# Causal mask added by VectorE in PSUM, and a layer norm with its turnings in two halves

## The reference

```
xn = (x - mean) / sqrt(var + 1e-05)
att = q @ k.T / sqrt(HD);  att = where(key > query, -inf, att);  y = softmax(att) @ v
x = x + (y @ wo) * silu(moe0(xn))          # layer 0
xn = layernorm(x)
x = x + delta_rule(xn) * silu(moe1(xn))    # layer 1
```

## Time and profile before

| what | value |
|---|---|
| median of 3 runs | 1938.27 us (1934.45 to 1939.06) |
| the profiled execution | 1930.35 us, span 1928.6 us |
| busy PE, DVE, ACT, POOL | 92%, 74%, 51%, 37% of the span |
| mean granted TensorE clock | 0.974 |
| ACT's idle time before the exponentials of attention | 17.8 us until a mask matmul, 12.9 us until a score matmul, 9.0 us unnamed |

### The profile page before, as it was taken

The page is one execution under the profiler, slowest core; times in us unless marked ns, Lnnn a source line. Parts: engine busy times, 40 slices in busy tenths (PEclk is TensorE's granted clock), DMA queues, the critical chain, the costliest instruction groups (busy, mean ns, idle before and its releaser), DMA issues.

```text
span 1928.6 us, 43598 instructions
## 1 busy us (share of the span) xinstructions
PE 1774.4 (92%) x14838; PEld 1284.5 (67%) x14838; DVE 1421.1 (74%) x2477; ACT 987.0 (51%) x2680; POOL 705.1 (37%) x870
## 2 busy tenths in 40 slices
PE   4578888899889999999999999999999999999997
PEld 3236665333545568777787787787877877877776
DVE  5776775111477578888888888888888888888887
ACT  1002223788522246566666565565665756656664
POOL 5640001120040224263362552643624616426334
PEclk9779998999989999999999999999999999999999
DMA  6725664010022310100100001001001010010010
GB/s 255 227 92 175 191 185 132 26 31 13 1 82 73 96 48 13 44 33 11 44 7 37 33 11 44 33 11 44 33 11 44 0 44 33 11 44 33 11 55 22
DMA packets 76374, 112.43 MB, mean 58 GB/s; under 512 B 24332, under 2 KB 57756, under 8 KB 73122
## 3 DMA queue, kind: packets, MB, share of 16 engines
q1 hardware_dynamic: 72810, 102.95, 16.1%
q0 software_dynamic: 3072, 8.39, 1.4%
q10 hardware_dynamic: 446, 0.48, 0.1%
HBM read 86.22 MB, written 28.73 MB: 60 GB/s over the span
## 4 chain that ended last, share of the span: by engine, by line
PE 55%; ACT 10%; issue 3%; DVE 3%; POOL 1%; DMA 0%; ACTq 0%; SPq 0%; POOLq 0%; DVEq 0%
PE ps L1344 9%; PE ps L1391 6%; PE ps L1401 4%; PE ps L1535 3%; PE ps L1638 3%; PE ps L1625 3%; PE ps L1640 3%; ACT gmask_Q L1780 2%; PE ps L1609 2%; PE ps L1614 2%; PE ps L1418 2%; PE ps L1428 2%; PE ps L1445 2%; PE ps L1597 2%; PE ps L1589 2%
## 5 line engine op out<-in xcount | busy, mean ns | idle before, releaser
L1860 POOL TENSOR_TENSOR kq_decayed<-conv,decay_rows 128x256 f32<-128x256 f32 x234 | 181.7, 801 | 452.2 <-PE ps L1638 452.2
L1989 DVE SCALAR_TENSOR_TENSOR conv<-raw,tap_st,conv 128x1024 f32<-128x1024 f32 x202 | 280.8, 1390 | 3.6
L1344 PE MATMUL ps<-xnT,w_conv_st 128*128 128x512 f32 x544 | 245.9, 596 | 0.0
L817 DVE TENSOR_REDUCE m_part<-ps 128x1 f32<-128x640 f32 (+7 forms) x176 | 176.1, 1027 | 67.8 <-PE ps L668 49.5
L1344 PEld LDWEIGHTS ps<-xnT,w_conv_st 128*128 128x128 f32 x544 | 98.2, 190 | 99.7 <-issue 94.9
L1020 ACT ACTIVATE probs<-ps 128x1024 f32<-128x1024 f32 (+1 forms) x192 | 142.1, 816 | 39.7 <-PE ps L944 17.8
L1401 PE MATMUL ps<-w_z_st,xnT 128*128 128x256 f32 x512 | 150.4, 396 | 0.0
L1659 ACT COPY raw<-ps 128x512 f32<-128x512 f32 x136 | 80.7, 593 | 123.3 <-PE ps L1344 122.5
L912 POOL DMA_INDIRECT slot_outputs<-scratch_slots_y,token_slots x32 | 30.4, 950 | 303.6 <-POOLq L497 207.4
L645 PE MATMUL ps<-k_stack,q_stack 128*128 128x512 bf16 (+3 forms) x384 | 103.3, 363 | 33.4 <-DVE m_part L817 18.1
L1391 PE MATMUL ps<-w_out_st,xn_nat 128*128 128x256 f32 x544 | 125.9, 384 | 6.9 <-ACT xn_nat L1692 6.9
(11 more groups left out here) (356 smaller groups left out, 4330.1 us busy)
## 6 DMA issues: line engine op xcount, KB each, us to landing
decay_rows<-scratch_egc SPq DMA_DIRECT2D x17, 1024.0 KB, 4.6
w_conv_st<-in_w_conv SPq DMA_DIRECT2D x17, 512.0 KB, 3.2
scratch_slots_x<-yacc SPq DMA_DIRECT2D x8, 1024.0 KB, 15.0
slot_rows<-scratch_slots_x SPq DMA_DIRECT2D x16, 512.0 KB, 4.9
scratch_slots_y<-slot_outputs SPq DMA_DIRECT2D x16, 512.0 KB, 3.7
w_gate_up<-in_gu SPq DMA_DIRECT2D x8, 768.0 KB
w_gate_up<-in_gu SPq DMA_DIRECT2D x32, 192.0 KB
k_nat_decayed<-in_gu SPq DMA_DIRECT2D x22, 256.0 KB, 2.8
```

What stands on the lines that cost most here:

```text
L817: dve.tensor_reduce(dst, src, AX.X, ALU.max).then_inc(s_max, 1)
L1344: mm = pe.matmul(ps[:, 6 + n % 2, :], wc[:, k, (n // 2) * P:(n // 2 + 1) * P], m.xnT[:, k, (n % 2) * HALF:(n % 2 + 1) * HALF], start=k == ...
L1860: op = g.tensor_tensor(kqe[:, e, :, at], cv[:, 0:2, at], egr[:, e, at].unsqueeze(1).broadcast_to([P, 2, P]), ALU.mult)
L1989: op = dve.scalar_tensor_tensor(out=cv[:, t, :], in0=raw[:, t, at:at + T], scalar=tap[:, t, at:at + 1], in1=cv[:, t, :], op0=ALU.mult, op1 ...
```

## The change

The mask matmul is taken out of PE's stream; a unit with a diagonal is finished by its score matmuls. DVE adds `future` to the first 128 columns of both banks in one operation of 128 x 2 x 128, in place in PSUM, and ACT's exponential of such a unit waits for that operation (`s_mk`) in place of PE. DVE's stream is laid out anew: the masks of each tile in order, the four operations that weight the expert outputs behind the masks of tiles 4 to 7 instead of at the start of the group, and the two masks of the next group's first tile ahead of the copy of this group's result.

The second layer norm runs in two halves of four chunks. DVE takes the statistics and aggregates of each half, POOL works on four columns at a time, and DVE normalises the first half behind the second half's aggregates. PE turns a half as soon as it is normalised, ACT copies 128x512 blocks, and the router matmuls of a half wait for its two blocks only. The first layer norm stays as it is.

```diff
+def dve_layer_norm_halves(dve, step, x, st, mv, xn, s_var, s_rstd, rstd):
+
+    for half in range(2):
+        of = range(half * NC // 2, (half + 1) * NC // 2)
+        for c in of:
+            step(dve.bn_stats(st[:, c, :], x[:, c, :]))
+        step.wait()
+        for c in of:
+            last = dve.bn_aggr(mv[:, c, :], st[:, c, :])
+        last.then_inc(s_var, 1)
+    for half in range(2):
+        dve.wait_ge(s_var, half + 1)
+        dve.wait_ge(s_rstd, half + 1)
+        for c in range(half * NC // 2, (half + 1) * NC // 2):
+            step(dve.tensor_scalar(xn[:, c, :], x[:, c, :], mv[:, c, 0:1], rstd[:, c:c + 1],
+                                   ALU.subtract, ALU.mult))
+
+def pool_rsqrt_var_halves(nc, pool, step, mv, rstd, minus_half, s_var, s_rstd):
+    for half in range(2):
+        of = slice(half * NC // 2, (half + 1) * NC // 2)
+        pool.wait_ge(s_var, half + 1)
+        step.link(nc.gpsimd.tensor_scalar(rstd[:, of], mv[:, of, 1], LN_EPS, None, ALU.add))
+        nc.gpsimd.tensor_tensor(rstd[:, of], rstd[:, of], minus_half[:, 0:1].broadcast_to([P, NC // 2]),
+                                ALU.pow).then_inc(s_rstd, 1)
...
-                                   m.qst[:, bass.ds(i * REP + 2 * pair + q, 1), at:at + w], start=True, stop=done > 0)
-                    if not done:
-                        mm = pe.matmul(ps[:, bank, 0:P], m.identb[:], m.future[:], start=False, stop=True)
+                                   m.qst[:, bass.ds(i * REP + 2 * pair + q, 1), at:at + w], start=True, stop=True)
...
-                        act.wait_ge(s_sc, i * UN + n + 1)
+                        if done:
+                            act.wait_ge(s_sc, i * UN + n + 1)
+                        else:
+                            act.wait_ge(s_mk, i * 2 * NC + 2 * kt + pair + 1)
...
+            def mask(i, kt):
+
+                for pair in range(REP // 2):
+                    n = unit(kt) + chunks(kt) * pair
+                    dve.wait_ge(s_sc, i * UN + n + 1)
+                    square = ps[:, 2 * (n % 3):2 * (n % 3) + 2, 0:P]
+                    dve.tensor_tensor(square, square, m.future[:].unsqueeze(1).broadcast_to([P, 2, P]), ALU.add).then_inc(s_mk, 1)
...
+            mask(0, 0)
             for i in range(NKV):
                 dve.wait_ge(s_pv, i * NC + 2)
                 dve.tensor_copy(vst[:], m.vaug[:, i, :, :]).then_inc(s_v, 1)
...
+                for kt in range(1, NC):
+                    mask(i, kt)
+                    if kt >= NC - TOP0:
+                        weigh(i, kt - (NC - TOP0))
+                if i + 1 < NKV:
+                    mask(i + 1, 0)
                 dve.wait_ge(s_pv, (i + 1) * NC + 2)
                 dve.tensor_copy(m.oT[:, i, :], ps[:, 6:8, :].rearrange("p b n -> p (b n)")).then_inc(s_o, 1)
...
-            pe.wait_ge(s_l1, 2 * NC)
-            for k in range(KT):
-                for c in range(NC):
-                    mm = pe.transpose(ps[:, 2 + 2 * k + c // 4, (c % 4) * P:(c % 4 + 1) * P],
-                                      m.xn[:, c, k * P:(k + 1) * P], m.ident[:])
-                mm.then_inc(s_tr, 1)
+            for half in range(2):
+                pe.wait_ge(s_l1, NC + (half + 1) * NC // 2)
+                for k in range(KT):
+                    for c in range(half * NC // 2, (half + 1) * NC // 2):
+                        mm = pe.transpose(ps[:, 2 + 2 * k + half, (c % 4) * P:(c % 4 + 1) * P],
+                                          m.xn[:, c, k * P:(k + 1) * P], m.ident[:])
+                    mm.then_inc(s_tr, 1)
             pe.wait_ge(in_r, 32)
-            pe.wait_ge(s_xnT, 2)
             for c in range(NC):
+                if c % 4 == 0:
+                    pe.wait_ge(s_xnT, KT + c // 4 * KT)
...
-            for k in range(KT):
-                act.wait_ge(s_tr, k + 1)
-                nc.scalar.copy(m.xnT[:, k, :], two_banks(2 + 2 * k)).then_inc(s_xnT, 1)
+            for half in range(2):
+                for k in range(KT):
+                    act.wait_ge(s_tr, half * KT + k + 1)
+                    nc.scalar.copy(m.xnT[:, k, half * HALF:(half + 1) * HALF], ps[:, 2 + 2 * k + half, :]).then_inc(s_xnT, 1)
```

More of the change, by code:

```diff
@@ L886, in stage_attention @@
                                               sem("yT_made"), sem("s_made"), sem("dve_steps"))
-        s_mixed = sem("pair_mixed")
+        s_mixed, s_mk = sem("pair_mixed"), sem("unit_masked")
         block = ctx.enter_context(nc.Block())
@@ L1033, in _, with weigh @@
             dve.sem_inc(s_o, 1)
+            def mask(i, kt):
[4 more added lines that the diff above has]
+                    dve.tensor_tensor(square, square, m.future[:].unsqueeze(1).broadcast_to([P, 2, P]), ALU.add).then_inc(s_mk, 1)
+            def weigh(i, n):
+                if n == 0:
+                    dve.wait_ge(s_got[i % 2], 16 * TOP0 * (i // 2 + 1))
+                    step.link(dve.tensor_scalar(m.yacc[:, i, :], got[:, i % 2, 0, :], m.wsel[:, i, 0:1], None, ALU.mult))
+                    return
+                op = dve.scalar_tensor_tensor(out=m.yacc[:, i, :], in0=got[:, i % 2, n, :], scalar=m.wsel[:, i, n:n + 1],
+                                              in1=m.yacc[:, i, :], op0=ALU.mult, op1=ALU.add)
+                if n < TOP0 - 1:
+                    step.link(op)
+                else:
+                    op.then_inc(s_mix, 1)
+            mask(0, 0)
             for i in range(NKV):
@@ L1874, in _ @@
             g.memset(w3f.rearrange("p c s -> p (c s)"), 0.0).then_inc(s_zero, 1)
-            pool_rsqrt_var(nc, pool, l1, m.mv, m.rstd, m.minus_half, s_lnv, s_lnr)
+            pool_rsqrt_var_halves(nc, pool, l1, m.mv, m.rstd, m.minus_half, s_lnv, s_lnr)
             pool.wait_ge(s_l1, 2 * NC)
@@ L2077, in _ @@
             beta = m.beta[:, 0:NV, :]
-            dve_layer_norm(dve, l1, m.x, m.st, m.mv, m.xn, s_lnv, s_lnr, m.rstd)
+            dve_layer_norm_halves(dve, l1, m.x, m.st, m.mv, m.xn, s_lnv, s_lnr, m.rstd)
             dve.wait_ge(in_w, 64)
```

## The result

The changed kernel takes 1925.04 us in the median of six runs (1920.01 to 1929.53), the kernel before 1936.26 us in six beside them (1933.76 to 1939.06). The ratio is 0.9938, 95% interval 0.9924 to 0.9952: 12.0 us faster, between 9.3 and 14.7. I had forecast 4.7 us, and named faster as the likeliest side. So the side is right and the size is about two and a half times the forecast.

The account below looks back on a forecast made before the run. Attention was taken as a PE-ACT-PE chain, the second layer norm as one serial chain, with PE the bound afterwards. Masks 0.8 plus layer norm 3.9 gave 4.7 us, from 1938.27 to 1933.6 us; range 1925 to 1941.

Parts of the forecast that it names:

- the rival with the shorter stall: First group of heads: four fewer gathers in a row shorten ACT's 8.37 us stall by 5.0 us, 1928.6; chance 0.25.
- The likeliest case: Whole kernel: masks 0.8 us plus layer norm 3.9 us, 4.7 us faster, 1933.6 us; chance 0.42.
- The layer norm, -3.9 us: Second layer norm in halves: router matmuls end at 542.15 in place of 546.04, 3.9 us earlier.
- The collision: Layer norm: first-half normalisations on DVE wait for POOL's second power over shared ports, costing about 0.5 us.
- The shift at 546 us: After the layer norm, rival: later DVE routing or weights eat some 3 of the 3.9 us, 1937; chance 0.08.
- The masks, -0.1 us a group: Attention: masks moved from PE to DVE gain 0.1 us a group, 0.8 us over eight.
- the detour: Masked units go PE, DVE, ACT: 0.51 us in place of a direct 0.04, 0.47 us extra latency.
- the end of the group: Attention, after the trades at tiles 5 to 7: PE is about 0.45 us ahead.
- The last step: Change of groups: the next group's first masked unit gives 0.47 - 0.11 us back.
- My slope for a longer detour: Attention: detour stands three times in a group's path, so each further 0.1 us costs 0.3 us a group.
- an addition of 0.68 us: Rival of a long detour: PSUM addition takes 0.68 us, attention loses 7 us, kernel 1941.7; chance 0.15.
- The rival of a falling clock: Attention: PE's clock drops from small waits, about 10 us more per group wholly at 1.2 GHz, 1943; chance 0.05.

Follow-up runs that it names:

- 1: Kernel before with only the second layer norm in halves, attention as before; ratio 0.9960 (0.9944 to 0.9975).
- 9: Kernel before with 39 added turnings of the identity on PE ahead of the second layer norm's turnings; ratio 0.9979 (0.9962 to 0.9997).
- 12: Kernel before, unchanged, profiled a second time; first projection 18.17 us after the statistics, no timed ratio given.
- 2: Kernel before with only the masks on DVE and the later weighting, serial second layer norm; ratio 0.9968 (0.9950 to 0.9987).
- 6: Kernel with masks on DVE and serial layer norm, plus a second addition ahead of each mask addition; ratio to the kernel before 1.0070 (1.0042 to 1.0099).
- 7: Kernel with masks on DVE and serial layer norm, but key tile 0's masks back on PE; ratio to the kernel before 0.9968 (0.9949 to 0.9988).
- 8: Changed kernel with the first eight gathers moved to the second group and weighting one group later; ratio to the kernel before 0.9938 (0.9909 to 0.9968).
- 3: Kernel before, masks on PE, with each chunk's weighting made to wait for its group's fourth product; ratio 1.0060 (1.0042 to 1.0077).
- 4: Changed kernel with four gathers in a row at the start in place of eight; ratio to the kernel before 0.9901 (0.9883 to 0.9918).
- 10: Changed kernel with four gathers in a row at the start and key tile 0's masks on PE; ratio to the kernel before 0.9888 (0.9865 to 0.9910).
- 11: Changed kernel with four gathers in a row, key tile 0's masks on PE and 24 turnings ahead of the layer norm's; ratio to before 0.9865 (0.9843 to 0.9886).
- 5: Kernel before without any mask, neither mask matmuls nor additions, exponential's scale divided by 256; ratio 0.9923 (0.9902 to 0.9945).

## Why the prediction was right on the side and wrong on the size

The measured 1925.04 us lies at the lowest edge of my range, the edge that I had drawn for the rival with the shorter stall, and 8.6 us below the 1933.6 of my sum. Of these 8.6 us 2.0 are the kernel before itself (1938.27 in three runs, 1936.26 in six). The rest comes from three terms of the sum that were too small, all to the same side, less 1.7 us that the sum did not have.

**The likeliest case left the first group as it was: the largest miss.** The step that failed is that my sum took this gain at nothing. I had it as the rival with a chance of 0.25 and 5.0 us. Measured, the first group went from 30.57 to 26.05 us, of which 0.34 belongs to the masks, so 4.2 us belong to the gathers. The length of the row decides: twelve gathers with masks on PE give holes of 8.37, 9.77, 8.46 and 8.37 us (before, 1, 9, 12), eight give 3.92, 3.87, 3.54, 3.91 and 3.66 with masks on DVE (after, 2, 6, 7, 8) and 4.19 with masks on PE (3), some with a second wait of about 2 us behind them, and four at a group's start give none (4, 10, 11). Without any mask twelve gave 5.23 and 2.73 us (5). Against the rival I had held that gathers ran without harm before 335 and that later sets of four cost nothing. Both are true and neither excludes it: the row begins with attention, and ACT gets on for 7 us before it stops. How gathers hold PE is not settled. The trace of after records the product of the first tile at 339.72 us and the scores behind it, for which ACT waits, at 341.57, but ACT gets them at 345.52. What holds them back in between no view shows. PE in time order, kernel after:

```profile
339.72 1.93 PE L955 MATMUL ps<-probs,v_stage 128*32 128x512 f32 x16
341.57 1.15 PE L968 MATMUL ps<-q_stack,k_stack 128*128 x6
```

**The layer norm, -3.9 us: right against one execution, too small against the kernel.** The pair of profiles gives -4.3. But my price of the serial form was a single execution's. When the clock rises behind the idle stretch differs from profile to profile, and the serial form is exposed to it. In its four profiles without masks on DVE (before, 3, 5, 12) the router takes 3.76 to 5.34 us and the projection comes 16.8 to 18.2 us after the statistics, 17.8 in the mean. In five of the halves (without 11) it is 4.1 to 4.5 and 12.3 to 12.8, 12.6 in the mean. That is -5.2 us. The step that failed is the one that took the 546.04 us of one execution, with "some 4.5 us" of low clock read from one mean of 0.68, as the serial form's end. The three serial profiles with masks on DVE (2, 6, 7) are slower still: each has its router at a clock of 0.50 throughout, 7.07 us, and its projection after 20.1 or 20.2 us. Whether the masks have a part in that, or three executions were unlucky, is not shown.

The clock is the cause of these differences: the same 32 matmuls take 3.76 us where it is 1.00 (before, 9) and 7.07 where it is 0.50 (2, 6, 7). In number 9, with PE at work in the idle stretch, the turnings run at the upper level as well, and the projection comes 2.6 us ahead of the mean of those four (15.2 to 17.8). Why the clock rises late in the serial form and not in the halves was not tried alone; PE idles 11.6 to 11.9 us in the one and 8.1 to 8.4 in the other.

Inside it the terms held: a power over four columns 1.06 and 1.04 us (I took 0.94), PE's start 4.86 us after the statistics (5.44 forecast), the projection 12.52 (12.93). The collision for which I counted 0.5 us did not come. Four normalisations took 1.36 us in a row from 534.46 while POOL's second power ran from 535.03. The Trainium skill, "SBUF — State Buffer", section "Who interferes with whom", says that when a VectorE operation in a 2-port mode meets a GpSimd operation, whichever issues first holds the shared ports for its whole instruction. The earlier trace rows bore that out beside a memset; beside a power of 128x4 these rows show no such block, and the measurement decides. In which mode a normalisation ran no view tells.

**The shift at 546 us is not eaten.** Against the profile of before 1.0 us was given back, and I had taken that for the cost of a later routing chain. Over the same four and five profiles the rest of the kernel takes 1384.0 us in the mean behind the serial form and 1383.4 behind the halves: nothing is given back.

**The masks, -0.1 us a group: measured -0.34.** The addition (0.43) and the detour were right, and so was the way through the group: at tile 5 ACT is 0.22 us earlier than before (440.95 - 424.50 = 16.45 us from the group's start, 440.14 - 423.47 = 16.67 before; 0.19 forecast). The step that failed is the end of the group, where I had PE 0.45 us ahead. With the first tile's masks on PE (number 7) it is 0.70 us ahead (21.43 - 20.73). In the kernel before PE is late there. Its product of tile 6, then the exponentials that this product waits for, on ACT:

```profile
443.57 0.64 PE L928 MATMUL ps<-probs,v_stage 128*32 128x256 f32 x8
```

```profile
442.01 1.09 ACT L1020 ACTIVATE probs<-ps 128x512 f32<-128x512 f32 x2 [0.36 <-PE ps L944]
```

The exponentials are done at 443.10, and PE comes 0.47 us later. I let the detours of tiles 6 and 7 cancel what PE wins by then; as I read these rows, they hid in that lag. Numbers 5 and 7 fit this: seven tiles with masks on DVE and the first on PE cost at most 20.73 - 20.28 = 0.45 us a group more than no mask at all, which is one detour and not two or three. The lag was not changed by itself. The last step, 0.36 us given back by the first masked unit of the next group, was exact (21.09 - 20.73). My slope for a longer detour, 0.3 us a group for 0.1 us, is below the 0.5 of number 6, part of which is DVE being full. My own sum has a slip there: by its slope an addition of 0.68 us loses 8 x (0.78 - 0.1) = 5.4 us, not 7. No run had such an addition.

**What I had not seen** is 1.7 us behind the last group, where the clock falls for 3.4 us in the changed kernel and in numbers 2, 4 and 7, and for 6.8 us in 6, but not in 8, 10 and 11. The rival of a falling clock had looked for it within the groups, where the clock stayed at 1.00. Its cause stays open.

**The sum.** From these profiles attention until the eighth group goes from 160.1 us (mean of before, 1, 9 and 12) to 152.5 (after and 2), -7.6; behind it come +1.7, -5.2 in the layer norm and -0.7 in the rest. That makes -11.8 us, beside the measured 12.0 (9.3 to 14.7).

## What to carry to other kernels

Profile the kernel before more than once, or treat its one profile as a draw: a stretch behind an idle PE cost 16.8 us in one profile of the same kernel and 18.2 in the next, and the gain of shortening it is the gain against the mean. When work is moved off the bound engine, move only what the path doesn't wait for: the masks of the first tile are better left on PE, by the profiles' period of 20.73 us against 21.09. And when a change moves a wait, follow the queue that the wait was holding back; here the four gathers that it kept out of the first group were worth 4.2 us, the masks of all eight groups 8 x 0.34.

## What the runs showed of the hardware that I had not expected

A row of eight or twelve indirect gathers on POOL, 1.25 us each, stops the chain of attention: in all eleven profiles with such a row ACT falls idle 6.9 to 8.0 us behind the row's first gather, in number 8 in the second group, and it goes on 0.6 to 2.2 us behind the last one; in number 5 it goes on once in between. The DMA engines are busy only 0.34 of the time meanwhile (338 to 342 us, kernel before). Four gathers at a group's start do no harm, four at a group's end cost 2.6 to 3.2 us (3). The cause is not known. An in-place addition in PSUM by DVE costs nearly the same as one with its result in SBUF (0.43 and 0.42 us for 128x256).
